# Chunk 0 of a fused layer kernel on one core: identity made by GpSimd, single-block first weights, and two blocks of the first token half moved ahead of the second half's transposes

## The chip, the core and the metric

The kernel runs on one core of a Trainium2 chip. The metric is the device time in microseconds (us) of one execution. The engines are PE (TensorE), DVE (VectorE), ACT (ScalarE), POOL (GpSimd) and SP (SyncE, which here issues nearly all DMAs).

## The reference

`x` is (2, 4096, 256) float32. It is normalised over its last axis to `xn` (no scale, no shift), and

```
out = x + branch(xn) + gelu(xn @ w1 + b1) @ w2 + b2
```

with `w1` 256x1024, `w2` 1024x256. The branch is a spectral filter along the 256 features whose coefficients come from one number (a fractal dimension of the first 1024 values of `xn`), followed by a 24-bit latent code that is corrected and projected back. In the kernel the filter becomes two small circulant matrices, made once from the fractal dimension.

## The kernel before, in words

The 8192 tokens are 16 chunks of 512. In each chunk the feed-forward part has 8 blocks of 128 hidden units. For block m, `up` (line 861) puts six matmuls of 512 columns into bank `m % 2` of `p_h`: the three terms `w1_hi*xT_hi`, `w1_lo*xT_hi`, `w1_hi*xT_lo`, each over two halves k of the features. ACT makes `h` from that bank (gelu, line 428) and its rounded part `h_hi` (line 436), DVE the rest `h_lo` (line 606), and `down` (line 891) sums into `p_f` with four matmuls for `h_hi` (line 904) and two for `h_lo` (line 909). Block m + 2 needs its bank free: `up` waits for `gelu_done` of block m. Every operand is split so into a rounded part `hi` (made by ACT) and a remainder `lo` (made by DVE after `hi`).

All engines' programs are written out by hand in order; each engine does what stands there, waiting on semaphores. Chunk 0 is a start of its own:

- SP issues, in order: three loads of the first rows of `x` (line 238), the identity (line 289), the first part of `w1` (blocks 0 and 1, line 242 through `load_w1(0)`), then the small inputs, the second part of `w1`, the constants, the first part of `w2`, the `x` of chunk 1, the last parts of `w1` and `w2`, the basis, and others. Then it waits in `spread_rows(1)` (lines 268 to 287) for POOL's reciprocal deviations of chunk 1, writes them and the means to DRAM (line 275, `rows_dram`) and reads them back, broadcast to all partitions (line 286, `rows_sb`).
- POOL clears a few tiles, `ones` among them (line 330), then makes the reciprocal deviations of chunk 0 in two halves of tokens (lines 346 and 351).
- DVE: statistics of the first rows (lines 750 to 762), `normalise(0)` and `normalise(1)` (line 743, into `xn0`, which is the memory of a `rows_sb`), `w1_part_lo(0)` (line 730), then `xT_lo` of both halves (line 765), `w1_part_lo(1)`, the first step of the fractal dimension (lines 777 to 781), `hidden_lo(0, 0)`, `w2_part_lo(0)` (line 736), more of the dimension (lines 785 to 788), `w1_part_lo(2)`, `hidden_lo(0, 1)`, and then the statistics of chunk 1 (line 564).
- ACT: `w1_part_hi(0)` (line 476), `xT_hi` of both halves (line 487), `w1_part_hi(1)`, then gelu and `h_hi` of block 0, `w2_part_hi(0)`, gelu and `h_hi` of block 1, `w1_part_hi(2)`, gelu of block 2 and so on.
- PE: 12 matmuls on zeros (line 1052), the wait for the identity, for each half of the tokens four transposes of 128x128 (line 1059) into `p_s`, then `up` of blocks 0 to 3. Block 0 is cut in two halves of 256 columns, all three terms of the first half ahead of those of the second. After block 2 stands a small sum for the fractal dimension (line 1046). Then `down` of block m and `up` of block m + 4 take turns.

Chunk 1 (`first_branch_chunk`) starts the branch; on PE its second group of latents (line 930) needs the bits of chunk 0 taken by DVE (line 611). From there the chunks repeat in a loop.

Of the kernel before, what the change touches and what calls it, by code (L numbers as in the profile page):

```python
# [8 lines left out]
ALU = mybir.AluOpType  # L9
# [11 lines left out]
HF = E // 2  # L21
HR = 4
BANK = 512
W1_PARTS = ((0, 2), (2, 4), (4, 6), (6, MB))
W1_LOADS = ((0, 2), (2, 4), (4, MB))
W2_PARTS = ((0, 2), (2, 4), (4, MB))
W2_LOADS = ((0, 4), (4, MB))
# [38 lines left out]
S_END = S_WEL + KB * LAT  # L66


def build(nc, x, xt, small, latent, w1, w2, ident, consts, basis, codes, out):
    ctx = ExitStack()  # L70
    with ctx:
        def sb(name, shape, dt):
# [5 lines left out]
        def sem(name):  # L78
            return ctx.enter_context(nc.semaphore(name))
# [91 lines left out]
        rows_in = [sem("rows_in_even"), sem("rows_in_odd")]  # L171
        w1_in = [sem(f"w1_in{i}") for i in range(len(W1_LOADS))]
        w2_in = [sem(f"w2_in{i}") for i in range(len(W2_LOADS))]
        id_in, con_in, basis_in, small_in = sem("id_in"), sem("con_in"), sem("basis_in"), sem("small_in")
        code_in, latent_in, stored = sem("code_in"), sem("latent_in"), sem("stored")
        idle_set, pool_set, word_set, cw_set, le_set = (sem("idle_set"), sem("pool_set"), sem("word_set"),
                                                        sem("cw_set"), sem("le_set"))
# [56 lines left out]
        def _(sp):  # L234
# [51 lines left out]
                sp.dma_start(rows_sb[par][:, :, :].rearrange("p a t -> p (a t)"),  # L286
                             rows_dram[par].rearrange("a t -> (a t)").partition_broadcast(P)).then_inc(rows_in[par], 16)

            sp.dma_start(id_sb[:], ident).then_inc(id_in, 16)
            load_w1(0)  # L290
            sp.dma_start(small_sb[:], small).then_inc(small_in, 16)
            load_w1(1)
# [33 lines left out]
        @block.gpsimd  # L326
        def _(pool):
            nc.gpsimd.memset(eps[:], LN_EPS).then_inc(pool_set, 1)
            nc.gpsimd.memset(minus_half[:], -0.5).then_inc(pool_set, 1)
            nc.gpsimd.memset(ones[:], 1.0).then_inc(pool_set, 1)  # L330
            nc.gpsimd.memset(cw[:].bitcast(F32), 0.0).then_inc(cw_set, 1)
            nc.gpsimd.memset(le3[:], 0.0).then_inc(le_set, 1)
            pool.wait_ge(pool_set, 3)
            links = [0]

            def then(ins):

                links[0] += 1
                ins.then_inc(pool_link, 1)
                pool.wait_ge(pool_link, links[0])  # L340

            def inverse_root(step, par, tiles=slice(0, CT), mean=True):


                pool.wait_ge(stat_done, step + 1)
                nc.gpsimd.tensor_tensor(var_eps[:, tiles], mv[par][:, tiles, 1], eps[:, tiles],  # L346
                                        ALU.add).then_inc(veps_done, 1)
                if mean:
                    nc.gpsimd.tensor_copy(row_nums[par][:, 0, tiles], mv[par][:, tiles, 0]).then_inc(mean_done, 1)
                pool.wait_ge(veps_done, step + 1)  # L350
                nc.gpsimd.tensor_tensor(row_nums[par][:, 1, tiles], var_eps[:, tiles], minus_half[:, tiles],  # L351
                                        ALU.pow).then_inc(rstd_done, 1)

            def turn(c):

                pool.wait_ge(scaled, c)
                pool.wait_ge(u_lo, c)
                for k, op in enumerate((ALU.add, ALU.subtract)):
                    nc.gpsimd.tensor_tensor(uv[:, k, :], xn[:, 0, :], xn[:, 1, :], op).then_inc(turned, 1)  # L359


            for g in range(2):
                inverse_root(g, 0, slice(g * HALF, (g + 1) * HALF), mean=False)
            inverse_root(1 + HEAD, 1)


            pool.wait_ge(angle_made, 1)
            wide = [P, PAIRS, COLS]
            t, s, s2, s4 = angle[:, :], powers[:, 0, :], powers[:, 1, :], powers[:, 2, :]
            odd = con[:, K_ODD:K_ODD + PAIRS * COLS].rearrange("p (n c) -> p n c", c=COLS)  # L370
            even = con[:, K_EVEN:K_EVEN + PAIRS * COLS].rearrange("p (n c) -> p n c", c=COLS)
            then(nc.gpsimd.tensor_tensor(s, t, t, ALU.mult))
            nc.gpsimd.tensor_tensor(s2, s, s, ALU.mult)
            then(nc.gpsimd.tensor_tensor(quads[:], odd, s.unsqueeze(1).broadcast_to(wide), ALU.mult))
            nc.gpsimd.tensor_tensor(s4, s2, s2, ALU.mult)
            then(nc.gpsimd.tensor_tensor(quads[:], quads[:], even, ALU.add))
            by_two = quads[:].rearrange("p (n two) c -> p n two c", two=2)
            nc.gpsimd.tensor_tensor(weighted[:], t, con[:, K_WK:K_WK + COLS], ALU.mult)
            then(nc.gpsimd.tensor_tensor(halves2[:], by_two[:, :, 1, :], s2.unsqueeze(1).broadcast_to([P, 2, COLS]),
                                         ALU.mult))  # L380
            then(nc.gpsimd.tensor_tensor(halves2[:], halves2[:], by_two[:, :, 0, :], ALU.add))
            then(nc.gpsimd.tensor_tensor(series[:], halves2[:, 1, :], s4, ALU.mult))
            then(nc.gpsimd.tensor_tensor(series[:], series[:], halves2[:, 0, :], ALU.add))
            then(nc.gpsimd.tensor_tensor(series[:], series[:], weighted[:], ALU.mult))
            nc.gpsimd.tensor_tensor(filt_w[:], series[:, 0:KB], series[:, KB:2 * KB], ALU.mult).then_inc(filt_made, 1)

            inverse_root(2 + HEAD, 0)
            turn(1)
            with pool.Fori(0, (CHUNKS - 4) // 2) as i:
                for u in range(2):  # L390
                    turn(2 * i + 2 + u)
                    inverse_root(2 * i + 3 + u + HEAD, 1 - u)
            turn(CHUNKS - 2)
            inverse_root(CHUNKS - 1 + HEAD, 1)
            turn(CHUNKS - 1)

        @block.scalar
        def _(act):
# [83 lines left out]


            w1_part_hi(0)
            for g in range(2):
                act.wait_ge(t0_done, g + 1)
                nc.scalar.copy(half_tokens(xT_hi[0], g), half_bank(g)).then_inc(t0_hi, 1)
            w1_part_hi(1)
            act.wait_ge(small_in, 16)
            gelu(0, 0, first=True)  # L490
            hidden_hi(0, 0, first=True)
            w2_part_hi(0)
            gelu(0, 1, first=True)
            hidden_hi(0, 1, first=True)
            w1_part_hi(2)
            gelu(0, 2, first=True)
            hidden_hi(0, 2, first=True)
            w2_part_hi(1)
            w1_part_hi(3)
            gelu(0, 3, first=True)  # L500
            hidden_hi(0, 3, first=True)
            w2_part_hi(2)
# [44 lines left out]
        def _(dve):  # L547
# [209 lines left out]
            last.then_inc(stats_made, 1)  # L757
            dve.wait_ge(stats_made, 2)
            aggregate(0, range(HALF, CT))
            for g in range(2):  # L760
                normalise(g)
            w1_part_lo(0)
            for g in range(2):
                dve.wait_ge(t0_hi, g + 1)
                nc.vector.tensor_tensor(half_tokens(xT_lo[0], g), half_bank(g), half_tokens(xT_hi[0], g).bitcast(F32),  # L765
                                        ALU.subtract).then_inc(t0_lo, 1)


            table = [P, NS, FRE]
# [1 line left out]
            logs = con[:, K_CLOG:K_CLOG + NS * FRE].rearrange("p (s f) -> p s f", f=FRE)  # L771
            numbers = con[:, K_NUM:K_NUM + FRE].unsqueeze(1).broadcast_to(table)
            values = fr_v[:, :].unsqueeze(1).broadcast_to(table)
            w1_part_lo(1)

            first_rows = p_s[:, :, :].rearrange("p g (a t) -> p (g a) t", t=P)[:, :, 0]
            nc.vector.tensor_copy(fr_v[:, :], first_rows).then_inc(fr_taken, 1)
# [8 lines left out]
            then(nc.vector.tensor_tensor(fr_b[:], values, fr_s[:, 1, :].unsqueeze(2).broadcast_to(table), ALU.is_gt))  # L786
            then(nc.vector.tensor_tensor(fr_a[:], fr_b[:], masks, ALU.mult))
            nc.vector.tensor_reduce(fr_s[:, 2, :], fr_a[:], AX.X, ALU.add).then_inc(part_counts, 1)
            w1_part_lo(2)
            hidden_lo(0, 1)  # L790
            statistics(1, 1)
            dve.wait_ge(stats_made, 3)
# [5 lines left out]
            then(nc.vector.tensor_tensor(fr_a[:], fr_b[:], logs, ALU.mult))  # L798
            nc.vector.tensor_reduce(fr_d[:, 0:1], fr_a[:].rearrange("p s f -> p (s f)"), AX.X,
                                    ALU.add).then_inc(logged, 1)  # L800
            w1_part_lo(3)
            w2_part_lo(1)
            hidden_lo(0, 3)
            dve.wait_ge(dim_made, 1)
# [53 lines left out]
        def _(pe):  # L858
            mm = nc.tensor.matmul

            def up(c, par, m, first=False):
# [4 lines left out]
                for n, (m0, _) in enumerate(W1_PARTS):  # L866
                    if first and m == m0:

                        pe.wait_ge(*((w1_hi_ready, 1) if n == 0 else (w1_ready, n + 1)))
                if not (first and m < 2):  # L870

                    pe.wait_ge(gelu_done, MB * c + m - 1)

                groups = 2 if first and m == 0 else 1
                for g in range(groups):
                    tok = slice(g * CTOK // groups, (g + 1) * CTOK // groups)
                    n = 0
                    for w, xp in ((w1_hi, xT_hi), (w1_lo, xT_hi), (w1_hi, xT_lo)):
                        if groups == 2:

                            if w is w1_lo and g == 0:
                                pe.wait_ge(w1_ready, 1)
                            elif w is w1_hi:
                                pe.wait_ge(t0_hi if xp is xT_hi else t0_lo, g + 1)
                        for k in range(KB):
                            last = mm(p_h[:, m % 2, tok], w[:, k, m * P:(m + 1) * P], xp[par][:, k, tok],  # L886
                                      start=(n == 0), stop=(n == 3 * KB - 1))
                            n += 1
                last.then_inc(up_done, 1)

            def down(c, m, first=False):

# [157 lines left out]
            pe.wait_ge(idle_set, 1)  # L1050
            for _ in range(IDLE):
                mm(p_f[:, 0, :], idle[:, 0:P], idle[:], start=True, stop=True)
            pe.wait_ge(id_in, 16)
            for g in range(2):

                pe.wait_ge(xn0_done, g + 1)
                for k in range(KB):
                    for j in range(HALF):
# [1 line left out]
                                                   xn0[:, g * HALF + j, k * P:(k + 1) * P], id_sb[:])  # L1060
                last.then_inc(t0_done, 1)

            pe.wait_ge(pool_set, 3)
            for m in range(LOOK):
                up(0, 0, m, first=True)
                if m == 2:
                    summed_over(0, NS, fr_s[:, 0, :], part_sums, fr_summed)
# [21 lines left out]
def constants():  # L1089
# [52 lines left out]
    for par in range(2):  # L1142
# [4 lines left out]
        fixed[2 * SEG, :, 0:LAT] = 9.5  # L1147
        fixed[ROWS:ROWS + SYN, :, 0:SYN] = (1.0 - 13.0 * np.eye(SYN))[:, None, :]
        codes[:, par, 0:ROWS] = fixed.reshape(P, ROWS)
    return np.eye(P, dtype=f4), con, basis, codes.reshape(P, 2 * P)  # L1150


def layouts(inputs):
# [37 lines left out]
```

## Time and profile before

| | us |
|---|---|
| median of 3 runs | 414.21 |
| the three runs | 413.71, 414.21, 415.49 |
| the profiled execution, its own time | 413.36 |
| span of the profiled execution | 411.5 |
| time around the span (413.36 - 411.5) | 1.86 |
| TensorE clock granted, mean of the span | 1.0 of full |

Times in the rows are from the start of the span. "Idle before" is the time in which an engine had nothing to do ahead of the instruction, with what released it. Back-to-back instructions of ACT and DVE overlap by about 0.1 us in the records, since the next starts while the last drains: a group's us are from its first start to its last end.

### The profile page before, as it was taken

How to read it: one execution, taken by the hardware profiler on the slowest of the kernel's cores; microseconds unless marked ns; L12 is line 12 of the kernel's file. 1: busy time of each engine (PE TensorE's matmuls, PEld its weight loads, DVE VectorE, ACT ScalarE, POOL GpSimd, SP SyncE). 2: the span in 40 equal slices, each digit the busy share in tenths (PEclk: the TensorE clock that was granted, in tenths of full speed). 3: DMA queues.
4: the chain of work that ended last, by engine and by line, in shares of the span. 5: the costliest groups of instructions: out<-in, count | busy, mean ns of one | idle time of the engine just before them, and what ended most of it. 6: DMA issues, size and time to landing. Idle time of an engine off the chain costs nothing.

```text
span 411.5 us, 5561 instructions
## 1 busy us (share of the span) xinstructions
PE 405.6 (99%) x1785; PEld 325.0 (79%) x1785; DVE 308.8 (75%) x505; ACT 218.4 (53%) x325; POOL 71.8 (17%) x100
## 2 busy tenths in 40 slices
PE   8999999999999999999999999999999999999996
PEld 4887788888878878788887878888788887878874
DVE  7889986868678686876968778686786868676654
ACT  3966536555454655536555454655536654464541
POOL 2143301212012121201212012121111212012000
PEclk9999999999999999999999999999999999999999
DMA  7544233222323113233113333213333111111011
GB/s 214 187 155 154 102 104 102 59 51 97 104 102 102 37 66 102 102 102 101 49 55 102 102 102 101 34 69 102 102 102 101 52 51 51 52 52 53 0 51 51
DMA packets 16495, 35.78 MB, mean 87 GB/s; under 512 B 5452, under 2 KB 8164, under 8 KB 16484
## 3 DMA queue, kind: packets, MB, share of 16 engines
q1 hardware_dynamic: 16340, 35.52, 27.0%
q10 hardware_dynamic: 144, 0.13, 0.1%
q8 instruction: 5, 0.08, 0.1%
q14 instruction: 6, 0.05, 0.0%
HBM read 27.19 MB, written 8.45 MB: 87 GB/s over the span
## 4 chain that ended last, share of the span: by engine, by line
PE 91%; DVE 4%; DMA 2%; POOL 1%; issue 1%; ACT 1%; SPq 0%; DVEq 0%; POOLq 0%
PE p_h L886 40%; PE p_f L904 26%; PE p_f L909 13%; PE p_s L941 5%; PE p_l L930 3%; PE p_s L960 2%; DMA rows_sb<-rows_dram 1%; PE p_g L954 1%; DMA x_sb<-x 1%; DMA rows_dram<-row_nums 1%; DVE stats L564 1%; POOL row_nums L351 1%; DVE h_lo L606 0%; DVE xn L586 0%; DVE xn L591 0%
## 5 line engine op out<-in xcount | busy, mean ns | idle before, releaser
L428 ACT ACTIVATE h<-p_h,small_sb 128x512 f32<-128x512 f32 x128 | 88.0, 688 | 155.4 <-PE p_h L886 155.3
L606 DVE TENSOR_TENSOR h_lo<-h,h_hi 128x512 fp32r<-128x512 f32 x128 | 90.1, 705 | 66.8 <-ACT h_hi L436 66.6
L904 PE MATMUL p_f<-h_hi,w_hi 128*128 128x512 f32 x254 | 99.3, 391 | 0.0
L904 PE MATMUL p_f<-h_hi,w_lo 128*128 128x512 f32 x254 | 98.9, 389 | 0.0
L886 PE MATMUL p_h<-xT_hi,w_hi 128*128 128x512 f32 (+1 forms) x258 | 85.7, 413 | 0.1
L436 ACT CAST h_hi<-h 128x512 fp32r<-128x512 f32 x128 | 79.5, 621 | 5.8
L886 PE MATMUL p_h<-xT_hi,w_lo 128*128 128x512 f32 (+1 forms) x258 | 79.4, 389 | 0.0
L886 PE MATMUL p_h<-xT_lo,w_hi 128*128 128x512 f32 (+1 forms) x258 | 79.1, 388 | 0.0
L909 PE MATMUL p_f<-h_lo,w_hi 128*128 128x512 f32 x254 | 78.2, 389 | 0.0
L359 POOL TENSOR_TENSOR uv<-xn 128x512 f32<-128x512 f32 x30 | 44.5, 1502 | 127.2 <-DVE xn L591 127.2
L886 PEld LDWEIGHTS p_h<-xT_lo,w_hi 128*128 128x128 f32 x258 | 48.3, 188 | 10.5 <-DVE xT_lo L765 0.2
L886 PEld LDWEIGHTS p_h<-xT_hi,w_lo 128*128 128x128 f32 x258 | 48.3, 188 | 10.2
L886 PEld LDWEIGHTS p_h<-xT_hi,w_hi 128*128 128x128 f32 x258 | 48.4, 189 | 10.1 <-issue 0.3
L909 PEld LDWEIGHTS p_f<-h_lo,w_hi 128*128 128x128 f32 x254 | 47.7, 188 | 10.1
L904 PEld LDWEIGHTS p_f<-h_hi,w_hi 128*128 128x128 f32 x254 | 47.7, 188 | 10.0
L904 PEld LDWEIGHTS p_f<-h_hi,w_lo 128*128 128x128 f32 x254 | 47.7, 188 | 9.9
L346 POOL TENSOR_TENSOR var_eps<-mv,eps 128x4 f32<-128x4 f32 (+1 forms) x17 | 3.8, 222 | 171.0 <-DVE mv L569 171.0
L596 DVE TENSOR_TENSOR xT_lo<-xn,xT_hi 128x1024 fp32r<-128x1024 f32 x15 | 32.7, 2179 | 0.5 <-ACT xT_hi L406 0.5
L630 DVE SCALAR_TENSOR_TENSOR xt_sb<-p_f,bias,xt_sb 128x512 f32 (+1 forms) x30 | 21.1, 745 | 12.3 <-PE p_f L909 12.3
L601 DVE TENSOR_TENSOR uv_lo<-uv,uv_hi 128x1024 fp32r<-128x1024 f32 x16 | 19.6, 1227 | 6.1 <-ACT uv_hi L413 6.1
L586 DVE TENSOR_TENSOR xn<-xt_sb,rows_sb 128x1024 f32<-128x1024 f32 x15 | 18.4, 1225 | 7.6 <-DMA rows_sb<-rows_dram 4.2
L406 ACT CAST xT_hi<-xn 128x1024 fp32r<-128x1024 f32 x15 | 15.8, 1054 | 15.3 <-DVE xn L591 15.3
(115 smaller groups left out, 326.5 us busy)
## 6 DMA issues: line engine op xcount, KB each, us to landing
xt_sb<-xt SPq DMA_DIRECT2D x16, 512.0 KB, 5.3
x_sb<-x SPq DMA_DIRECT2D x15, 512.0 KB, 4.7
rows_sb<-rows_dram SPq DMA_DIRECT2D x15, 512.0 KB, 4.4
out<-xt_sb SPq DMA_DIRECT2D x15, 512.0 KB, 2.9
xt_sb<-w SPq DMA_DIRECT2D x3, 512.0 KB, 7.6
xt_sb<-w SPq DMA_DIRECT2D x2, 256.0 KB, 4.5
x_sb<-x SPq DMA_DIRECT2D x2, 128.0 KB, 2.4
x_sb<-x SPq DMA_DIRECT2D x1, 256.0 KB, 3.0
```

The costliest lines, as they stand in the source:

```text
L359: nc.gpsimd.tensor_tensor(uv[:, k, :], xn[:, 0, :], xn[:, 1, :], op).then_inc(turned, 1)
L428: nc.scalar.activation(h[m % 2][:], p_h[:, m % 2, :], ACT.Gelu, bias=small_sb[:, S_B1 + m:S_B1 + m + 1]).then_inc(gelu_done, 1)
L436: nc.scalar.copy(h_hi[m % HR][:], h[m % 2][:]).then_inc(h_hi_done, 1)
L586: nc.vector.tensor_tensor(xn[:, :, :], columns(c), to_halves(rows_sb[par][:, 0, :]), ALU.subtract).then_inc(centred, 1)
L596: nc.vector.tensor_tensor(xT_lo[par][:, :, :], xn[:, :, :], xT_hi[par][:, :, :].bitcast(F32), ALU.subtract).then_inc(t_lo, 1)
L601: nc.vector.tensor_tensor(uv_lo[:, :, :], uv[:, :, :], uv_hi[:, :, :].bitcast(F32), ALU.subtract).then_inc(u_lo, 1)
L606: nc.vector.tensor_tensor(h_lo[m % HR][:], h[m % 2][:], h_hi[m % HR][:].bitcast(F32), ALU.subtract).then_inc(h_lo_done, 1)
L630: nc.vector.scalar_tensor_tensor(out=xc, in0=p_f[:, k, :], scalar=bias[:, k:k + 1], in1=xc, op0=ALU.add, op1=ALU.add).then_inc(ffn_added, 1)
L886: last = mm(p_h[:, m % 2, tok], w[:, k, m * P:(m + 1) * P], xp[par][:, k, tok], start=(n == 0), stop=(n == 3 * KB - 1))
L904: mm(p_f[:, a, :], w[:, m, a * HF:(a + 1) * HF], h_hi[r][:], start=(m == 0 and w is w2_hi), stop=False, skip_group_check=True)
L909: last = mm(p_f[:, a, :], w2_hi[:, m, a * HF:(a + 1) * HF], h_lo[r][:], start=False, stop=(m == MB - 1), skip_group_check=True)
L941: last = mm(p_s[:, k, :], w[:, k, :], xp[:, k, :], start=(n == 0), stop=False, skip_group_check=True)
```

## The change

SP no longer loads an identity; POOL makes it from `ones` with an `affine_select` of 128x128 after its clearing. The first part of `w1` (still one load) is rounded in two parts of one block each. On PE, the first half of the tokens is transposed, then the first two terms of block 0 on that half, then the second half is transposed, then the rest of block 0 and all of block 1 on the first half, then both blocks on the second half. On DVE, `w1_part_lo(0)` moves in between `normalise(0)` and `normalise(1)`, and the new `w1_part_lo(1)` stands between the `xT_lo` of the two halves.

```diff
-W1_PARTS = ((0, 2), (2, 4), (4, 6), (6, MB))
+W1_PARTS = ((0, 1), (1, 2), (2, 4), (4, 6), (6, MB))
...
-            sp.dma_start(id_sb[:], ident).then_inc(id_in, 16)
             load_w1(0)
...
             pool.wait_ge(pool_set, 3)
+
+            nc.gpsimd.affine_select(out=id_sb[:], in_=ones[:], pattern=[[1, P]], base=0, channel_multiplier=-1,
+                                    compare_op=ALU.is_equal, fill=0.0).then_inc(id_made, 1)
...
             w1_part_hi(0)
+            w1_part_hi(1)
             for g in range(2):
                 act.wait_ge(t0_done, g + 1)
                 nc.scalar.copy(half_tokens(xT_hi[0], g), half_bank(g)).then_inc(t0_hi, 1)
-            w1_part_hi(1)
+            w1_part_hi(2)
...
-            for g in range(2):
-                normalise(g)
+            normalise(0)
             w1_part_lo(0)
+            normalise(1)
             for g in range(2):
                 dve.wait_ge(t0_hi, g + 1)
                 nc.vector.tensor_tensor(half_tokens(xT_lo[0], g), half_bank(g), half_tokens(xT_hi[0], g).bitcast(F32),
                                         ALU.subtract).then_inc(t0_lo, 1)
+                if g == 0:
+                    w1_part_lo(1)
...
+            def half_up(m, g, terms):
+
+                tok = slice(g * GTOK, (g + 1) * GTOK)
+                for n in terms:
+                    w, xp = ((w1_hi, xT_hi), (w1_lo, xT_hi), (w1_hi, xT_lo))[n]
+                    for k in range(KB):
+                        last = mm(p_h[:, m, tok], w[:, k, m * P:(m + 1) * P], xp[0][:, k, tok],
+                                  start=(n == 0 and k == 0), stop=(n == 2 and k == KB - 1))
+                return last
...
-            pe.wait_ge(id_in, 16)
+            pe.wait_ge(id_made, 1)
...
+            turn_rows(0)
+            pe.wait_ge(w1_hi_ready, 1)
+            pe.wait_ge(t0_hi, 1)
+            half_up(0, 0, (0,))
+            pe.wait_ge(w1_ready, 1)
+            half_up(0, 0, (1,))
+            turn_rows(1)
+            pe.wait_ge(t0_lo, 1)
+            half_up(0, 0, (2,))
+            pe.wait_ge(w1_ready, 2)
+            half_up(1, 0, (0, 1, 2))
+            pe.wait_ge(t0_hi, 2)
+            half_up(0, 1, (0, 1))
+            pe.wait_ge(t0_lo, 2)
+            half_up(0, 1, (2,)).then_inc(up_done, 1)
+            half_up(1, 1, (0, 1, 2)).then_inc(up_done, 1)
+
             pe.wait_ge(pool_set, 3)
-            for m in range(LOOK):
+            for m in range(2, LOOK):
                 up(0, 0, m, first=True)
```

The other parts of `w1` keep their places under numbers one higher, and `up` of block 0 loses its own cut in two.

## Rows read from the trace of the kernel before

**Rows 1.** The profile's page: busy us, share of the span and instructions of each engine.

```profile
PE 405.6 (99%) x1785; PEld 325.0 (79%) x1785; DVE 308.8 (75%) x505; ACT 218.4 (53%) x325; POOL 71.8 (17%) x100
```

**Rows 2.** The chain that ended last, first 40 us: start us, us, what.

```profile
13.12 0.13 PE p_g L1046 x2
...
13.28 0.18 DVE fr_s L785
...
15.43 1.32 DVE stats L564 x4
...
21.53 4.40 DMA rows_sb<-rows_dram
...
37.98 1.20 PE p_l L930 x4
```

**Rows 3.** Who waited for whom, first 45 us: us in total, times, longest.

```profile
PE p_l L930 <- DVE word L611: 0.4, 1, 0.4
```

**Rows 4.** Timeline of PE: start us, us, engine, line, operation, count, idle before.

```profile
6.74 0.63 PE L1059 MATMUL p_s<-id_sb,rows_sb 128*128 128x128 f32 x4 [0.33 <-DVE rows_sb L743]
7.65 0.66 PE L1059 MATMUL p_s<-id_sb,rows_sb 128*128 128x128 f32 x4 [0.29 <-DVE rows_sb L743]
8.41 0.48 PE L886 MATMUL p_h<-xT_hi,w_hi 128*128 128x256 f32 x2
...
9.74 0.40 PE L886 MATMUL p_h<-xT_hi,w_lo 128*128 128x256 f32 x2
9.97 0.40 PE L886 MATMUL p_h<-xT_lo,w_hi 128*128 128x256 f32 x2
...
11.60 0.61 PE L886 MATMUL p_h<-xT_hi,w_hi 128*128 128x512 f32 x2
...
13.10 0.70 PE L886 MATMUL p_h<-xT_hi,w_hi 128*128 128x512 f32 x2
```

**Rows 5.** Timeline of ACT, the same columns.

```profile
7.16 0.62 ACT L476 CAST w_hi<-xt_sb 128x512 fp32r<-128x512 f32 x1 [4.93 <-DMA xt_sb<-w]
7.68 1.25 ACT L487 CAST xT_hi<-p_s 128x512 fp32r<-128x512 f32 x2
...
10.48 0.69 ACT L428 ACTIVATE h<-p_h,small_sb 128x512 f32<-128x512 f32 x1 [1.03 <-PE p_h L886]
...
12.24 0.68 ACT L428 ACTIVATE h<-p_h,small_sb 128x512 f32<-128x512 f32 x1
...
29.76 0.38 ACT L525 CAST c_hi<-p_l 128x256 fp32r<-128x256 f32 x1
```

**Rows 6.** Timeline of DVE, the same columns.

```profile
6.18 0.41 DVE L743 TENSOR_SCALAR rows_sb<-x_sb,mv,row_nums 128x256 f32<-128x256 f32 x1
6.86 0.73 DVE L743 TENSOR_SCALAR rows_sb<-x_sb,mv,row_nums 128x256 f32<-128x256 f32 x2 [0.27 <-POOL row_nums L351]
7.81 0.69 DVE L730 TENSOR_TENSOR w_lo<-xt_sb,w_hi 128x512 fp32r<-128x512 f32 x1 [0.21 <-ACT w_hi L476]
8.42 1.28 DVE L765 TENSOR_TENSOR xT_lo<-p_s,xT_hi 128x512 fp32r<-128x512 f32 x2
...
11.85 0.69 DVE L606 TENSOR_TENSOR h_lo<-h,h_hi 128x512 fp32r<-128x512 f32 x1 [1.01 <-ACT h_hi L436]
...
31.97 0.42 DVE L836 TENSOR_TENSOR c_lo<-c_f,c_hi 128x256 fp32r<-128x256 f32 x1
```

**Rows 7.** Timeline of SP's queue, the same columns.

```profile
2.11 0.43 SPq L289 DMA_DIRECT2D id_sb<-ident  x1
2.58 0.43 SPq L242 DMA_DIRECT2D xt_sb<-w  x1
```

**Rows 8.** Groups of POOL by form: busy us, mean ns | idle before us, releaser.

```profile
L351 POOL TENSOR_TENSOR row_nums<-var_eps,minus_half 128x4 f32<-128x4 f32 x15 | 15.3, 1019 | 0.0
...
L351 POOL TENSOR_TENSOR row_nums<-var_eps,minus_half 128x2 f32<-128x2 f32 x2 | 1.5, 736 | 0.2
...
L346 POOL TENSOR_TENSOR var_eps<-mv,eps 128x2 f32<-128x2 f32 x2 | 0.4, 196 | 3.3 <-DVE mv L569 3.3
...
L330 POOL MEMSET ones<- 128x128 f32 x1 | 0.2, 205 | 0.0
```

More of the change, by code:

```diff
@@ L66, with build @@
 S_END = S_WEL + KB * LAT
-def build(nc, x, xt, small, latent, w1, w2, ident, consts, basis, codes, out):
+def build(nc, x, xt, small, latent, w1, w2, consts, basis, codes, out):
     ctx = ExitStack()
@@ L173, in build @@
         w2_in = [sem(f"w2_in{i}") for i in range(len(W2_LOADS))]
-        id_in, con_in, basis_in, small_in = sem("id_in"), sem("con_in"), sem("basis_in"), sem("small_in")
+        id_made, con_in, basis_in, small_in = sem("id_made"), sem("con_in"), sem("basis_in"), sem("small_in")
         code_in, latent_in, stored = sem("code_in"), sem("latent_in"), sem("stored")
@@ L494, in _ @@
             hidden_hi(0, 1, first=True)
-            w1_part_hi(2)
+            w1_part_hi(3)
             gelu(0, 2, first=True)
@@ L498, in _ @@
             w2_part_hi(1)
-            w1_part_hi(3)
+            w1_part_hi(4)
             gelu(0, 3, first=True)
@@ L773, in _ @@
             values = fr_v[:, :].unsqueeze(1).broadcast_to(table)
-            w1_part_lo(1)
+            w1_part_lo(2)
             first_rows = p_s[:, :, :].rearrange("p g (a t) -> p (g a) t", t=P)[:, :, 0]
@@ L788, in _ @@
             nc.vector.tensor_reduce(fr_s[:, 2, :], fr_a[:], AX.X, ALU.add).then_inc(part_counts, 1)
-            w1_part_lo(2)
+            w1_part_lo(3)
             hidden_lo(0, 1)
@@ L800, in _ @@
                                     ALU.add).then_inc(logged, 1)
-            w1_part_lo(3)
+            w1_part_lo(4)
             w2_part_lo(1)
@@ L867, in up @@
                     if first and m == m0:
-                        pe.wait_ge(*((w1_hi_ready, 1) if n == 0 else (w1_ready, n + 1)))
+                        pe.wait_ge(w1_ready, n + 1)
                 if not (first and m < 2):
                     pe.wait_ge(gelu_done, MB * c + m - 1)
[L874 to L888, printed above, removed]
-                last.then_inc(up_done, 1)
+                n = 0
+                for w, xp in ((w1_hi, xT_hi), (w1_lo, xT_hi), (w1_hi, xT_lo)):
+                    for k in range(KB):
+                        last = mm(p_h[:, m % 2, :], w[:, k, m * P:(m + 1) * P], xp[par][:, k, :],
+                                  start=(n == 0), stop=(n == 3 * KB - 1))
+                        n += 1
+                last.then_inc(up_done, 1)
+            def half_up(m, g, terms):
+                tok = slice(g * GTOK, (g + 1) * GTOK)
+                for n in terms:
+                    w, xp = ((w1_hi, xT_hi), (w1_lo, xT_hi), (w1_hi, xT_lo))[n]
+                    for k in range(KB):
+                        last = mm(p_h[:, m, tok], w[:, k, m * P:(m + 1) * P], xp[0][:, k, tok],
+                                  start=(n == 0 and k == 0), stop=(n == 2 and k == KB - 1))
+                return last
             def down(c, m, first=False):
@@ L1052, in _, with turn_rows @@
                 mm(p_f[:, 0, :], idle[:, 0:P], idle[:], start=True, stop=True)
-            pe.wait_ge(id_in, 16)
-            for g in range(2):
+            pe.wait_ge(id_made, 1)
+            def turn_rows(g):
                 pe.wait_ge(xn0_done, g + 1)
@@ L1149, in constants @@
         codes[:, par, 0:ROWS] = fixed.reshape(P, ROWS)
-    return np.eye(P, dtype=f4), con, basis, codes.reshape(P, 2 * P)
+    return con, basis, codes.reshape(P, 2 * P)
 def layouts(inputs):
@@ L1178 @@
     arrays = {name: np.ascontiguousarray(a) for name, a in layouts(inputs).items()}
-    for name, a in zip(("ident", "consts", "basis", "codes"), constants()):
+    for name, a in zip(("consts", "basis", "codes"), constants()):
         arrays[name] = a
```

## The prediction

> **What bounds the kernel now.** I read the page's busy shares first: PE is busy for 405.6 of 411.5 us [rows 1], so a change of chunk 0 can only matter by what it does to the few waits before the steady part. Next the chain that ended last, in order of time [rows 2]. It leaves PE at 13.25 us, after block 2 and the small sum for the fractal dimension: DVE work, from 13.28 to the statistics of chunk 1 at 15.43, then the trip of the row numbers through DRAM (the read back alone 4.40 us, landing at 25.93), more DVE, and back to PE at 37.98 us. From there PE carries it nearly alone. In the list of waits PE's idle time at that place is 0.4 us, for DVE's bits of chunk 0 [rows 3]. So from 13.3 to 38 us it is DVE's chain, not PE's, that sets the end, with PE only 0.4 us ahead of it. Whatever delays DVE at 13 to 15 us goes into the time in full; whatever PE gains there is lost in the wait at 38 us.
>
> Then, by the timelines, what starts DVE's chain. At 11.85 DVE begins `hidden_lo(0, 0)` after 1.01 us of idling for ACT's `h_hi` [rows 6]; behind it stand `w2_part_lo(0)` and then the step of 13.28, which PE's sum (over at 13.25) released at the same moment [rows 2]. ACT in turn begins the gelu of block 0 at 10.48 after 1.03 us of idling for PE [rows 5], and from there works without a gap (the gelu of block 1 follows at 12.24, with two casts between, and its later casts feed `w1_part_lo(2)` and `hidden_lo(0, 1)`, which DVE has between 13.28 and 15.43). So ACT from 10.48 on is a solid line, and **the number that decides is when PE completes block 0**: its last two matmuls start at 9.97 and end at 10.37, ACT starts 0.11 later [rows 4, 5].
>
> **The change part by part.**
>
> *Identity load gone.* Each DMA behind it leaves SP 2.58 - 2.11 = 0.47 us earlier [rows 7]. Only one is waited for: the first part of `w1`, for which ACT idles until 7.16 [rows 5]. Its landing can come between 0 us (if the transfers ahead of it set it) and 0.47 us earlier; I take 0.4, as it stands right behind the identity in the queue, so ACT starts at 6.76. Everything behind gains the same and nobody waits for it.
>
> *Identity by GpSimd.* The trace has no `affine_select`. From below the nearest row is the clearing of `ones`, 0.2 us for the same 128x128; from above the power function, whose 736 ns for two columns and 1019 ns for four make 0.14 us a column, 18 us for 128 [rows 8]. The cover is POOL's idle time of 3.3 us before its first `var_eps` [rows 8]: PE needs the identity only at 6.7. I take a cost of nothing: a select has no function to evaluate and is nearest the clearing. POOL takes no more than 3.3 us unless it goes by the power function's price, which is kept as a rival. The Trainium skill speaks against using this engine: "GPSIMD Engine Reference", section "Elementwise — side-by-side cycle accounting", gives about 12 cycles an element where code branches on data; by its 1.2 GHz that would be an estimated 1.3 us here, which no row shows and which the cover would still hide.
>
> *Single blocks.* ACT's cast of 512 columns takes 0.62 and steps by 0.52 (7.16 to 7.68); one of 256 takes 0.38 [rows 5], and steps by about 0.3. Two of them: 6.76 and 7.06, ends 7.15 and 7.45. ACT is free for the first `xT_hi` at 7.36; the first transposes end at 7.37 as before [rows 4]. So `xT_hi` of the first half runs 7.41 to 7.99, where it was 7.68 to 8.26: 0.27 gained.
>
> *DVE's order.* `normalise(0)` ends at 6.18 + 0.41 = 6.59 [rows 6]. `w1_part_lo(0)`, now ahead of `normalise(1)`, waits for ACT until 7.15 and takes 0.42 (the row of 256 columns [rows 6]), stepping by 0.34. `normalise(1)`, queued behind that wait, runs 7.52 to 8.25 instead of 6.86 to 7.59 [rows 6]: 0.66 later. Who waits: the second transposes. Then `xT_lo` of the first half from 8.17 to 8.85, `w1_part_lo(1)` from 8.77 to 9.19.
>
> *PE.* First half, terms 0 and 1 of block 0: from 8.05 (0.06 after `xT_hi`). A pair of 256-column matmuls steps by 9.97 - 9.74 = 0.23 [rows 4], so they are issued by 8.52. The second transposes go 8.52 to 9.18 (0.66 [rows 4]), against an end of 8.31 before. The next matmul came 0.10 after the transposes' end before (8.31 to 8.41); I take 0.07: 9.25. Term 2 of block 0: to 9.48. Block 1 on the first half: 0.70, to 10.18. Meanwhile ACT makes the second `xT_hi` 9.22 to 9.80 and DVE the second `xT_lo` 9.84 to 10.52; both are ready in time for PE: terms 0 and 1 of block 0's second half to 10.65, and term 2 from 10.65, ending 0.40 after [rows 4] at 11.05. **Block 0 is complete at 11.05 instead of 10.37: 0.68 later.** The reason is plain counting: 18 half matmuls and four transposes now stand between the first `xT_hi` and the end of block 0, where 12 half matmuls did. Block 1 then ends its issue at 11.35, a little ahead of the 11.60 of before (24 half matmuls at 0.117 are 2.8 us either way): PE has filled its gaps, but block 2 cannot use it, since its bank waits for the gelu of block 0: 11.16 + 0.69 = 11.85, then 0.05, so 11.9 against 11.60. Block 3 waits for the gelu of block 1 at 12.24 + 0.68 + 0.68 = 13.60 and starts at 13.65 against 13.10 [rows 4, 5]. PE itself is 0.55 late.
>
> *DVE's chain.* `h_lo` at 11.85 + 0.68 = 12.53, then `w2_part_lo(0)`, so the step of 13.28 comes at about 13.9; the casts that DVE needs next come 0.68 later too. Chunk 1's statistics move from 15.43 to 16.1, POOL idles before its next turn so nothing absorbs it, SP sends the numbers when POOL is done, and the return to PE moves from 37.98 to 38.65. PE's 0.55 fits under it (its wait there grows from 0.44 to 0.57).
>
> **Sum.** -0.27 (`xT_hi` sooner, from the load and the smaller cast) and +0.95 (six more half matmuls, 0.70, and the transposes with their joint, 0.76, ahead of block 0's end, less the 0.5 of waits on PE that go) = +0.68 on DVE's chain, taken as +0.7. Against the profiled execution: 413.36 + 0.7 = 414.1 (span 412.2). The median lay 0.85 above that execution, so the forecast is 414.21 + 0.7 = **414.9**. The unknowns: a `w1` landing at the full 0.47 changes nothing below +0.6, as the first transposes then set the start; with faster joints +0.4 is the low end. With no earlier landing all steps after 7.4 come 0.35 later: +1.05. About 0.5% (2.1 us) is what a measurement of this kernel tells from no change.
>
> **The rivals.**
>
> *1. The delay is absorbed (chance 0.17).* Between 15 and 38 us something not in my chain, such as the landing of the row numbers among the other loads, would set DVE's pace. Against it: the read back lies on the chain itself [rows 2] and is issued only when the numbers are there. For it: 4.40 us for such a transfer is long enough to hide a queue. Time: +0, 414.2.
>
> *2. The overlap works (0.08).* If the first part of `w1` landed far sooner and the joints vanished, PE's filled gaps would count: block 1 done 0.25 to 0.5 us earlier. It needs block 0 complete by 10.37, for which PE would have to begin its half matmuls before 7.4, when the first transposes end. It could only come by if the wait of 0.4 us at 38 us went as well. Time: 413.8.
>
> *3. The identity becomes the bound, slower (0.03).* If the select goes at the power function's 0.14 us a column, POOL's first `var_eps`, which stands behind it, comes 18 - 3.3 = 14.7 us later [rows 8], and all of chunk 0 with it: 428.9. It decides from a duration of 3.3 us on. Were it between, say 6 us, the loss is 2.7.
>
> *4. The change doesn't do what it says (0.02).* Were the `w1` load not earlier and the second transposes held by another wait yet, PE would only do the same work in another order with +1.5: 415.7.
>
> **How the numbers follow.** The forecast has 0.70; its own range is +0.4 to +1.05, 414.6 to 415.3. Rivals 1 and 2 reach down to 413.8; a median moves by some tenths by itself (the three runs lie between 0.5 below and 1.3 above theirs), so the range is 413.5 to 416.1. All cases but the third lie within 2.1 us of 414.21, so "same" has 0.92; slower by over 0.5% takes the third case and a high draw on the forecast, 0.06; faster 0.02.
>
> **What would show it.** Right: ACT's first cast at 6.7 to 6.8; DVE's second `normalise` near 7.5; the first `xT_hi` near 7.4; the gelu of block 0 near 11.2; PE idle before block 2 and again before block 3; statistics of chunk 1 near 16.1; the latents at 38.6. Wrong: the gelu of block 0 at or before 10.5; a select of over 3.3 us; statistics late but the latents at 38.0 (rival 1).

## The result, and the profile after

| | before | after |
|---|---|---|
| median of 22 runs, us | 413.54 | 414.62 |
| lowest to highest | 412.95 to 415.49 | 413.83 to 415.91 |
| the profiled execution, its own time | 413.36 | 415.85 |
| its span | 411.5 | 414.1 |
| mean granted TensorE clock of its span | 1.000 | 0.996 |

The ratio is 1.0027, 95% interval 1.0019 to 1.0035: slower by 0.8 to 1.45 us, 1.08 by the medians. The forecast was +0.7 us with 0.92 on a change of less than 0.5%. The direction came, the change is 0.27%, and 414.62 lies in the range (413.5 to 416.1). The size was low: 1.08 against 0.70, just above the forecast's own +0.4 to +1.05. That 414.62 is so near the forecast of 414.9 is in part luck: the forecast stood on a median of three runs, 414.21, which was 0.67 above that of 22. The profiled execution is one of the slower ones and shows more than the typical loss, for a reason that comes below. Two executions of the kernel before, timed beside the experiments, took 576 and 698 us at mean clocks of 0.67 and 0.60; they belong to a slow state and stand in no comparison.

The identity first. The timeline of POOL in the changed kernel (start us, us, engine, line, operation, idle before; these columns hold for all timelines here):

```profile
1.61 0.29 POOL L334 TENSOR_SCALAR_AFFINE_SELECT id_sb<-ones 128x128 f32<-128x128 f32 x1
...
6.82 1.08 POOL L353 TENSOR_TENSOR row_nums<-var_eps,minus_half 128x2 f32<-128x2 f32 x1
```

The select took 0.29 us, near the clearing of `ones` [rows 8], five us before PE needs it. The second line is the power function for the second half of the tokens; it comes back below. Next, DVE from 5 to 12 us:

```profile
5.36 0.75 DVE L759 BATCH_NORM_STATS2 stats<-x_sb 128x6 f32<-128x256 f32 x2 [1.20 <-DMA x_sb<-x]
...
6.31 0.70 DVE L746 TENSOR_SCALAR rows_sb<-x_sb,mv,row_nums 128x256 f32<-128x256 f32 x2
6.93 0.42 DVE L733 TENSOR_TENSOR w_lo<-xt_sb,w_hi 128x256 fp32r<-128x256 f32 x1
7.94 0.73 DVE L746 TENSOR_SCALAR rows_sb<-x_sb,mv,row_nums 128x256 f32<-128x256 f32 x2 [0.59 <-POOL row_nums L353]
```

and ACT:

```profile
6.01 0.71 ACT L478 CAST w_hi<-xt_sb 128x256 fp32r<-128x256 f32 x2 [3.72 <-DMA xt_sb<-w]
7.82 0.59 ACT L490 CAST xT_hi<-p_s 128x512 fp32r<-128x512 f32 x1 [1.10 <-PE p_s L1065]
...
10.43 0.59 ACT L490 CAST xT_hi<-p_s 128x512 fp32r<-128x512 f32 x1 [2.02 <-PE p_s L1065]
...
13.02 0.69 ACT L430 ACTIVATE h<-p_h,small_sb 128x512 f32<-128x512 f32 x1 [1.49 <-PE p_h L893]
```

Against [rows 5] the first cast of `w1` starts 1.15 us sooner (6.01 for 7.16), but nobody gains by it. DVE waited 1.20 us for the last rows of `x` and took them at 5.36; it is those rows, not `w1`, that the first transposes now wait for. DVE takes them in before it normalises the first half, so the first transposes are late as well, and `normalise(1)` starts at 7.94, released by POOL's numbers, which took 1.08 us where the kernel before has 0.76 for the same operation (6.07 to 6.83), and not, as I had it, by `w1_part_lo(0)`, which was over at 7.35. Then PE, against [rows 4]:

```profile
7.16 0.63 PE L1065 MATMUL p_s<-id_sb,rows_sb 128*128 128x128 f32 x4 [1.12 <-DVE rows_sb L746]
...
8.55 0.56 PE L893 MATMUL p_h<-xT_hi,w_hi 128*128 128x256 f32 x2 [0.77 <-ACT xT_hi L490]
...
9.34 1.05 PE L1065 MATMUL p_s<-id_sb,rows_sb 128*128 128x128 f32 x4
...
11.05 0.63 PE L893 MATMUL p_h<-xT_hi,w_lo 128*128 128x256 f32 x2
11.48 0.63 PE L893 MATMUL p_h<-xT_lo,w_hi 128*128 128x256 f32 x2
...
12.52 0.40 PE L893 MATMUL p_h<-xT_lo,w_hi 128*128 128x256 f32 x2
12.76 0.40 PE L893 MATMUL p_h<-xT_hi,w_hi 128*128 128x256 f32 x2
```

A pair of half matmuls steps by 0.43 (11.05 to 11.48) where it steps by 0.24 a microsecond later. The windows say why; columns are busy us (instructions) of PE, weight loads, DVE, ACT and POOL, the granted clock, the share and the GB/s of the DMA engines:

```profile
8.00:9.00 1.00, 0.45 (x3) 0.48 (x4) 1.00 (x3) 0.41 (x1) 0.00 (x0) 0.90 1.04 325
9.00:10.00 1.00, 1.00 (x7) 1.00 (x7) 0.60 (x2) 0.00 (x0) 0.00 (x0) 0.50 1.02 385
10.00:12.00 2.00, 2.00 (x11) 2.00 (x10) 0.95 (x2) 1.10 (x2) 0.00 (x0) 0.50 1.04 391
12.00:14.00 2.00, 1.78 (x14) 1.61 (x14) 0.81 (x4) 0.94 (x2) 0.00 (x0) 0.95 1.06 365
```

From about 8.8 to 12.2 us the granted clock is 0.50, the 1.2 GHz level. Ahead of that PE had idled 1.12 us, done four transposes, and idled 0.77 us. From 14 us to the end it is 1.00, the 2.4 GHz level.

Last, the return to PE, in the chain (start us, us, what) and in the list of waits (us in total, times, longest):

```profile
40.57 1.19 PE p_l L936 x4
```

```profile
PE p_l L936 <- DVE word L614: 0.6, 1, 0.6
```

It is at 40.57 for 37.98 [rows 2], 2.59 later; the gelu of block 0 (13.02 for 10.48) is 2.54 later, the span 2.6 longer. PE's wait there grew from 0.4 [rows 3] to 0.6.

### The profile page after: what moved, and what is told of

It is laid out like the page before. It is cut to its first block, busy times and chain, and to the rows that moved or that the text cites. A ratio compares the mean times of both kernels' runs of the same rounds, so it can differ in the third digit from the quotient of the medians.

```text
span 414.1 us, 5560 instructions
## 1 busy us (share of the span) xinstructions
PE 406.7 (98%) x1776; PEld 326.8 (79%) x1791; DVE 308.6 (75%) x506; ACT 218.6 (53%) x326; POOL 74.3 (18%) x101
## 4 chain that ended last, share of the span: by engine, by line
PE 90%; DVE 4%; POOL 2%; ACT 2%; DMA 1%; issue 1%; SPq 0%; DVEq 0%; ACTq 0%
PE p_h L882 39%; PE p_f L910 26%; PE p_f L915 13%; PE p_s L947 5%; PE p_l L936 3%; PE p_s L966 2%; DMA x_sb<-x 1%; PE p_h L893 1%; DVE stats L567 1%; DVE h_lo L609 1%; PE p_s L1065 0%; ACT h L430 0%; DVE w_lo L733 0%; DVE xT_lo L599 0%; DVE uv L839 0%
## 5 line engine op out<-in xcount | busy, mean ns | idle before, releaser
L882 PE MATMUL p_h<-xT_hi,w_hi 128*128 128x512 f32 x252 | 84.3, 415 | 0.2 <-ACT h L430 0.2
L882 PE MATMUL p_h<-xT_hi,w_lo 128*128 128x512 f32 x252 | 77.9, 391 | 0.0
L882 PE MATMUL p_h<-xT_lo,w_hi 128*128 128x512 f32 x252 | 77.6, 389 | 0.0
L882 PEld LDWEIGHTS p_h<-xT_hi,w_hi 128*128 128x128 f32 x252 | 47.4, 189 | 10.1 <-issue 0.4
L882 PEld LDWEIGHTS p_h<-xT_lo,w_hi 128*128 128x128 f32 x252 | 47.3, 188 | 10.2
L882 PEld LDWEIGHTS p_h<-xT_hi,w_lo 128*128 128x128 f32 x252 | 47.3, 188 | 10.1
```

The lines of the kernel that those rows point to most:

```text
L882: last = mm(p_h[:, m % 2, :], w[:, k, m * P:(m + 1) * P], xp[par][:, k, :], start=(n == 0), stop=(n == 3 * KB - 1))
```

## The experiments

Each was timed in turn with the kernel before (9 to 12 runs of each; 32, 34 and 34 of the kernel before, medians 413.58, 413.53 and 413.62 in the three sets). "Fallen" means an execution whose mean clock is under 0.9965; the ratios and medians have all executions in them where nothing else is said. Three questions: does the end of block 0 set the whole time; which part of the change makes it late; what do the clock and the loads add.

**First set.** Edits against the changed kernel, except the last, which is against the kernel before.

`block0_first`: PE completes block 0 before block 1.

```diff
             half_up(0, 0, (2,))
-            pe.wait_ge(w1_ready, 2)
-            half_up(1, 0, (0, 1, 2))
             pe.wait_ge(t0_hi, 2)
             half_up(0, 1, (0, 1))
             pe.wait_ge(t0_lo, 2)
             half_up(0, 1, (2,)).then_inc(up_done, 1)
+            pe.wait_ge(w1_ready, 2)
+            half_up(1, 0, (0, 1, 2))
             half_up(1, 1, (0, 1, 2)).then_inc(up_done, 1)
```

> The changed kernel, but PE completes block 0 (both token halves) before any matmul of block 1. If the loss comes from the late completion of block 0 (theory 1), the gelu of block 0 starts about 0.7 us sooner than in the changed kernel and the median falls by about 0.7 us, to a ratio of 1.0000 to 1.0010 against the kernel before. If the loss comes from TensorE's clock falling in a third of the executions (theory 2), the order of the blocks changes nothing and the ratio stays at 1.0020 or more, with as many executions below a mean clock of 1.0 as in the changed kernel.

Measured 414.65, ratio 1.0043 (1.0022 to 1.0063). My main term was wrong: nothing was gained. Nor is the clock behind that: 5 of 11 executions had fallen, two of them to 0.992 (417.59 and 417.93 us), but the six others have a median of 414.41, where the changed kernel's 15 others have 414.33. The trace shows PE idle where the six half matmuls had stood:

```profile
10.40 0.51 PE L893 MATMUL p_h<-xT_hi,w_hi 128*128 128x256 f32 x2 [0.44 <-ACT xT_hi L490]
```

The second token half arrives too late whatever PE does meanwhile.

`after_warm`: filler work in PE's wait.

```diff
             turn_rows(0)
+            for _ in range(4):
+                mm(p_f[:, 0, 0:GTOK], idle[:, 0:P], idle[:, 0:GTOK], start=True, stop=True)
             pe.wait_ge(w1_hi_ready, 1)
```

> The changed kernel with four more matmuls of 256 columns on zeros behind the first transposes, where PE waits for the first xT_hi. Theory 2 (clock): hardly an execution has a mean clock below 1.0, and the median falls by 0.3 to 0.5 us, the upper tail by 1.3 us. Theory 1 (order): the median stays within 0.2 us of the changed kernel, ratio 1.0020 to 1.0030.

Measured 414.38, ratio 1.0023 (1.0006 to 1.0041). One of 9 executions had fallen, against 7 of 22. The median is 0.24 lower, between what the two theories said, and the interval does not tell it from no change; the eight others have 414.35, the same as the changed kernel's 414.33. So the filler gives back only what the falls cost. Its trace is at full clock and shows what the new order does without a fall:

```profile
8.91 0.60 PE L1065 MATMUL p_s<-id_sb,rows_sb 128*128 128x128 f32 x4
9.26 0.48 PE L893 MATMUL p_h<-xT_lo,w_hi 128*128 128x256 f32 x2
...
10.91 0.50 PE L893 MATMUL p_h<-xT_lo,w_hi 128*128 128x256 f32 x2
```

```profile
10.16 0.69 DVE L768 TENSOR_TENSOR xT_lo<-p_s,xT_hi 128x512 fp32r<-128x512 f32 x1 [0.75 <-ACT xT_hi L490]
```

The second `xT_lo` ends at 10.85, and the last term of block 0, which needs it, follows at 10.91; the gelu follows at 11.52.

`after_id_dma`: the identity by DMA again, at its old place.

```diff
+            sp.dma_start(id_sb[:], ident).then_inc(id_made, 16)
             load_w1(0)
...
-            nc.gpsimd.affine_select(out=id_sb[:], in_=ones[:], pattern=[[1, P]], base=0, channel_multiplier=-1,
-                                    compare_op=ALU.is_equal, fill=0.0).then_inc(id_made, 1)
...
-            pe.wait_ge(id_made, 1)
+            pe.wait_ge(id_made, 16)
```

> The changed kernel with the identity loaded by DMA again, as before the change. If taking that load away lets the first part of w1 compete with the last rows of x (theory 3: in the changed kernel those rows were used from 5.36 us instead of 4.66), the rows come at 4.7 again, the first transposes start near 6.7, w1 arrives near 7.1, and the time falls by 0 to 0.5 us against the changed kernel. If the removed load was the gain that I took it for, the time rises by 0.3 us.

Measured 414.17, ratio 1.0015 (1.0006 to 1.0024): less than the changed kernel, not more, though the two intervals overlap. DVE took the last rows at 4.67, as in the kernel before. None of the 11 executions had fallen; against the changed kernel's 15 at full clock (414.33) the gain is 0.16, and the rest of the 0.45 is the falls that did not come.

`id_only`: the kernel before with only the identity moved to GpSimd.

> The kernel before with the identity made by GpSimd and its load gone, nothing else. By my sum the first w1 cast starts 0.4 us sooner or more, the first xT_hi 0.2 us sooner, ratio 0.9993 to 1.0000. By theory 3 the last rows of x come 0.7 us later, the second transposes with them, and the ratio is 1.0005 to 1.0015.

Measured 413.66, ratio 1.0007 (0.9998 to 1.0017), the last rows of `x` taken at 5.00. The interval holds no change as well as theory 3's loss; the first `xT_hi` gained nothing (7.63 for 7.68).

**Second set.**

`dve_order`: DVE's `normalise(1)` ahead of `w1_part_lo(0)` again.

```diff
             normalise(0)
+            normalise(1)
             w1_part_lo(0)
-            normalise(1)
```

> The changed kernel with DVE's order of before: normalise(1) ahead of w1_part_lo(0). Theory A (what sets the end of block 0 is the chain of the second token half: second transposes, xT_hi, xT_lo; and what delays it is PE's own order, which holds the second transposes behind the first xT_hi): nothing changes within 0.2 us, since PE reaches the second transposes only at about 9 us anyway. Theory B (normalise(1) held by the wait for ACT's first cast is what delays it): the second transposes start 0.4 us sooner and the time falls by 0.4 us.

Measured 414.43, ratio 1.0026 (1.0014 to 1.0038): no change, theory A (the ten executions that had not fallen: 414.30). In its trace `normalise(1)` does start sooner, 2.24 us after the rows of `x` (7.07 after 4.83) instead of 2.59 (7.75 after 5.16 in `after_warm`), but PE comes to the second transposes only at 8.57. The gelu is 0.34 us earlier than `after_warm`, all of it from rows of `x` that came 0.33 sooner.

`together`: this, and both groups of transposes back to back on PE.

```diff
             turn_rows(0)
+            turn_rows(1)
             pe.wait_ge(w1_hi_ready, 1)
             pe.wait_ge(t0_hi, 1)
             half_up(0, 0, (0,))
             pe.wait_ge(w1_ready, 1)
             half_up(0, 0, (1,))
-            turn_rows(1)
             pe.wait_ge(t0_lo, 1)
```

> The changed kernel with both groups of transposes back to back as before, on PE and on DVE (identity by GpSimd, single blocks and both blocks of the first half first stay). Theory A: the second transposes start at about 8.0 us, the gelu of block 0 at 11.0 to 11.3 instead of 11.5, the time falls by 0.3 to 0.5 us, and executions with a fallen clock become rare, since PE no longer idles as long before its first half matmuls. If the six half matmuls of block 1 ahead of block 0's end are the loss, as my sum had it, nothing is gained.

Measured 414.21, ratio 1.0026 (1.0014 to 1.0038). The ratio did not fall, and fallen clocks did not become rare: 5 of 12. The seven others have a median of 414.08 where the changed kernel's 15 others have 414.33: 0.25 less, which is small beside the scatter of these few executions.

`together_first_dma`: `together`, `block0_first` and the identity's load in one.

> As the last, and block 0 completed ahead of block 1, and the identity loaded by DMA: of the change only the single-block weights and a block 1 cut in halves stay. Theory A with the x rows in time (theory 3): the gelu of block 0 starts at 10.3 to 10.6 as in the kernel before, ratio 0.9993 to 1.0007.

Measured 413.56, ratio 1.0006 (0.9997 to 1.0014); the gelu of block 0 at 10.62, 0.02 above what was expected, with the rows of `x` at 4.92. The whole loss is gone within what can be told.

`id_small_first`: `id_only`, and the small inputs loaded ahead of the first `w1`.

```diff
-            load_w1(0)
             sp.dma_start(small_sb[:], small).then_inc(small_in, 16)
+            load_w1(0)
```

> The kernel before with the identity by GpSimd, and the load of the small inputs put ahead of the first part of w1, where the identity's load stood. Theory 3 (w1 moved up competes with the last rows of x): those rows are used from 4.7 us as before, w1 arrives near 7, ratio 0.9993 to 1.0003, that is 0.2 to 0.3 us less than with the identity's load merely gone (1.0007). Against it: the rows still come at 5.0 or later.

Measured 413.64, ratio 1.0007 (0.9994 to 1.0020). In the trace the theory is right (rows at 4.68, `w1` cast at 7.13, span 411.3, the shortest of all), in the time nothing is shown.

**Third set.**

`together_first`: `together` and `block0_first`, identity by GpSimd.

> Transposes back to back as before and block 0 completed ahead of block 1, identity still by GpSimd. If the order of the transposes and the six half matmuls of block 1 are two delays of about 0.6 us side by side (each hides the other, so undoing one alone gained nothing), both are gone here: the gelu of block 0 starts 5.7 us after DVE takes the last rows of x, as in the kernel before (5.8), where the changed order needs 6.4. Ratio 1.0005 to 1.0015, the rest being the later rows of x. If only the identity's load made the difference in the run with it, the ratio stays at 1.002.

Measured 413.81, ratio 1.0001 (0.9992 to 1.0009), better than expected in the ratio. Its one trace is of an execution with a fallen clock (0.996), so its interval from the rows to the gelu, 6.61, can't be compared.

`together_first_small`: as the last, small inputs first.

> As together_first, with the load of the small inputs ahead of the first part of w1. If w1 moved up is what makes the last rows of x late, they come at 4.7 us and the ratio is 0.9990 to 1.0005, the best of all versions. If not, it equals together_first.

Measured 413.72, ratio 1.0001 (0.9989 to 1.0012): no better, so whether the small load's place is worth anything stays open. The rows came at 4.59, but `w1` at 7.80, so here ACT waited for `w1`:

```profile
7.80 0.71 ACT L478 CAST w_hi<-xt_sb 128x256 fp32r<-128x256 f32 x2 [5.51 <-DMA xt_sb<-w]
```

`together_warm`: `together` with four filler matmuls between the two groups of transposes.

> The run with the transposes back to back, in which 5 of 12 executions had a mean clock of 0.996, with four matmuls of 256 columns on zeros between the two groups of transposes. If PE's idling there makes the clock fall, 0 to 2 of 12 executions fall and the median is 414.1. If the fall has another cause, 3 to 6 of 12 fall.

Measured 414.20, ratio 1.0011 (1.0001 to 1.0021): 0 of 11 executions fell, the highest 414.61 where `together` had 415.87. The two were timed in different sets, but in this set `after_small_first`, without filler, fell in 4 of 11.

`after_small_first`: the changed kernel, small inputs first.

> The changed kernel with the load of the small inputs ahead of the first part of w1. Theory 3 for the changed kernel: the last rows of x come at 4.7 us instead of 5.36, w1 near 6.9 as with the identity's load kept, and the median falls to that run's 414.2 (ratio 1.0015). If the place of w1 in the queue does not matter, it stays at 1.0025.

Measured 414.57, ratio 1.0030 (1.0013 to 1.0046). The rows came at 4.62, as expected, and `w1` at 6.48, sooner than the 6.9 expected; the median did not fall: 4 of 11 executions had the fallen clock (median 416.13, the seven others 414.43).

**All traces side by side** (us, one execution each: when DVE takes the last rows of `x`, when ACT starts on `w1`, when the second transposes and the gelu of block 0 start):

| kernel | rows of x | w1 | 2nd transposes | gelu 0 | span | gelu - rows | span - gelu |
|---|---|---|---|---|---|---|---|
| before | 4.66 | 7.16 | 7.65 | 10.48 | 411.5 | 5.82 | 401.0 |
| id_small_first | 4.68 | 7.13 | 7.71 | 10.44 | 411.3 | 5.76 | 400.9 |
| id_only | 5.00 | 5.69 | 8.04 | 10.71 | 411.9 | 5.71 | 401.2 |
| together_first_dma | 4.92 | 6.54 | 7.95 | 10.62 | 411.7 | 5.70 | 401.1 |
| together_warm | 5.05 | 5.76 | 8.10 | 11.16 | 412.1 | 6.11 | 400.9 |
| dve_order | 4.83 | 5.50 | 8.57 | 11.18 | 412.1 | 6.35 | 400.9 |
| after_warm | 5.16 | 5.85 | 8.91 | 11.52 | 412.6 | 6.36 | 401.1 |
| block0_first | 5.38 | 6.12 | 9.13 | 11.74 | 412.9 | 6.36 | 401.2 |
| after_small_first | 4.62 | 6.48 | 8.37 | 10.98 | 412.1 | 6.36 | 401.1 |
| after_id_dma | 4.67 | 6.91 | 8.79 | 11.40 | 412.3 | 6.73 | 400.9 |
| together_first_small | 4.59 | 7.80 | 7.63 | 11.32 | 412.3 | 6.73 | 401.0 |
| together_first, fallen clock | 5.33 | 6.04 | 8.37 | 11.94 | 413.2 | 6.61 | 401.3 |
| together, fallen clock | 5.17 | 5.85 | 8.21 | 12.66 | 414.1 | 7.49 | 401.4 |
| after, fallen clock | 5.36 | 6.01 | 9.34 | 13.02 | 414.1 | 7.66 | 401.1 |

The last column is the finding that carries the rest: whatever was done to the first 13 us, the span ended 400.9 to 401.4 us after the gelu of block 0 began.

The columns before it show what makes that gelu late. In the five traces at full clock with the changed order on PE (`dve_order`, `after_warm`, `block0_first`, `after_small_first`, `after_id_dma`) it starts 2.61 us after the second transposes, to the hundredth, with block 1 ahead of block 0's end or behind it. So there it is the second half's own chain that sets it. The second transposes in turn start 3.74 or 3.75 us after the rows of `x` in four of the five (4.12 in `after_id_dma`, where `w1` is late), and 3.03 to 3.05 after them in `id_only`, `together_first_dma` and `together_warm`, where they are back to back. Each row is one execution, and when the rows of `x` come moves by some tenths between executions.

And the executions by clock. A mean does not say where the clock fell; the three traces of fallen executions (`after`, `together`, `together_first`) have the 0.50 from between 8.4 and 8.8 us to about 12 and 1.00 from 12.5 us on:

| kernels | fallen |
|---|---|
| before (the three sets) | 0 of 32, 0 of 34, 0 of 34 |
| after | 7 of 22 |
| block0_first, dve_order, together, after_small_first | 5 of 11, 2 of 12, 5 of 12, 4 of 11 |
| after_id_dma | 0 of 11 |
| after_warm, together_warm | 1 of 9, 0 of 11 |
| id_only, id_small_first | 1 of 12, 1 of 11 |
| together_first, together_first_dma, together_first_small | 2 of 12, 1 of 11, 1 of 12 |

In the changed kernel the 7 have a median of 415.63, the 15 others 414.33: a fall costs 1.3 us. One of the two counted for `together_first` has a mean of 0.949 and took only 414.10 us, so it is no such fall. The traces fit: from the rows of `x` to the gelu it is 7.66 us in the changed kernel's fallen execution and 6.36 in `after_warm`; in 3.4 us at half clock PE gets through what takes it 1.7 at full clock, and a part of the difference lies in waits.

## Why the prediction was right, and where it was wrong

- **"The number that decides is when PE completes block 0": shown.** The span less the gelu's start is the same within 0.5 us in 14 kernels, over a spread of 2.6 us in that start.
- **"+0.68 on DVE's chain, taken as +0.7": near for executions with the full clock, but by another sum, so in part by luck.** The 15 such executions have a median of 414.33, 0.8 above 413.54. In traces, from before to `after_warm`, the gelu moves by 1.04: 0.50 since the rows of `x` come later, 0.65 by the order on PE (6.36 from rows to gelu where `id_only` has 5.71), less 0.11 since `w1` is no longer waited for (5.71 for 5.82).
- **The term "six more half matmuls, 0.70": wrong as a term.** Undoing it alone (`block0_first`) left 6.36 us from rows to gelu, the same as with it. The second token half's own chain, second transposes, `xT_hi`, `xT_lo`, ended at the same time: PE holds the second transposes behind its wait for the first `xT_hi`. In the sum both ran beside each other and I had even written that `xT_lo` was ready at 10.52 for a use at 10.65; I should have read from this that removing the matmuls would gain 0.13. Undoing the transposes alone gained 0.25 (`together_warm`, 6.11), both together 0.66 (`together_first_dma`, 5.70).
- **The term "the transposes with their joint, 0.76": right in place, wrong in size.** That the second transposes now come later is what costs the time. But they hold PE for 0.35 us (8.91 to 9.26 in `after_warm`), not 0.76: the 8.41 in the kernel before is 0.15 after the end of `xT_hi`, which PE waited for, as its 8.55 in the changed kernel is 0.14 after that end. With 0.35 in the sum PE would have been ready for the last term some tenths earlier, and the second `xT_lo` (10.52) alone would have set the end. The total came out because my sum had the two paths only 0.13 apart.
- **The term "-0.27, `xT_hi` sooner": did not come.** The first `xT_hi` started at 7.82 in the changed kernel, 7.63 in `after_warm` and 7.85 in `block0_first`, against 7.68 before and 7.41 forecast. I took the identity's load to be only in the way of `w1`. `w1` did come sooner, by more than the 0.47 that I had as the most. But it then ran beside the last rows of `x`: over the eight traces in which `w1` follows those rows at once they were taken at 4.83 to 5.38, mean 5.16; over the six in which a smaller load stands between, at 4.59 to 4.92, mean 4.69. So the first transposes were late, which my sum held fixed at 6.74 to 7.37. What this costs in the median is not settled: restoring the load gained 0.45 in the changed kernel, of which 0.16 is left among executions at full clock, and moving the small load there gained nothing, though its one trace has the rows in time. In the kernel before, taking the load away cost nothing that can be told (1.0007, 0.9998 to 1.0017).
- **"`normalise(1)`, queued behind that wait": not the cause.** The new order does make it about 0.35 later after the rows of `x`, but PE is not there yet, and `dve_order` changed nothing in the time. In the changed kernel POOL's numbers released it. They were late themselves: this operation took 1.08 or 1.09 us in the three traces in which `w1_part_lo(0)` runs beside it (`after`, `after_warm`, `block0_first`) and 0.75 or 0.76 in the eleven others. That the one slows the other is argued from this alone.
- **Block 2 waits for the gelu, and PE's wait at 38 us grows from 0.44 to 0.57: the waits are there, the growth is not clear.** The list of waits has 0.2 before block 2. For the bits the fallen execution has 0.6, but the traces at full clock have 0.54 (`after_warm`) and 0.42 (`dve_order`).
- **What the sum left out: the clock.** My timeline left PE idle from 7.37 to 8.05 us and asked only when it was ready again. In a third of the executions TensorE's clock fell; where a trace shows it, it fell to the 1.2 GHz level right behind that idle time. That is about 0.4 us on the mean, and 0.29 of the 1.08 in the median (414.62 against 414.33). Filler in the idle time makes it rare (1 of 20 executions with it, 12 of 34 in the two kernels without). The Trainium skill, "TensorE: Matmul & The Clock Gate", section "HAM oscillation — how this bites in real kernels", warns of gaps in PE's work as the cause of such falls; the gaps here, 1.12 and 0.77 us, were shorter than the waits of its example, and a fall came all the same. The same two gaps stand in the trace of `dve_order`, whose clock stayed at 1.00. Why `after_id_dma`, with gaps of 1.07 and 1.06 us, had no fall in 11 stays open.
- **The rivals.** Absorbed (0.17): no, the last column of the table excludes it. The overlap works (0.08): no; PE filled its gaps and waited for the gelu. The identity as the bound (0.03): no, the select took 0.29 us, also far below the prediction's estimate of 1.3. The change not doing what it says (0.02): no; `w1` came sooner, and the second transposes stood behind the wait that the new order gives them.

No version beat the kernel before. The best, with its orders of transposes and blocks restored, equal it: 1.0001 (0.9992 to 1.0009, `together_first`) and 1.0006 (0.9997 to 1.0014, `together_first_dma`), where the changed kernel has 1.0027 (1.0019 to 1.0035). So the new order, with the falls that come with it, is shown as the cause of the loss; how it divides to the hundredth is read from single traces.

## What to carry to other kernels

Find the first handoff that a solid line of work hangs on (here the first gelu) and judge a reordering by that one time; filling PE's gaps with work that the next engine is not waiting for delays it. When two delays run beside each other, undoing one shows nothing: undo both before a cause is dismissed. Taking a load out of a queue moves the others up, also against the one ahead of them that everything waits for.

## What the runs showed of the hardware that was not expected

- An `affine_select` of 128x128 float32 on GpSimd took 0.29 us, hardly more than the 0.20 of a clearing.
- With a DMA of 256 KB issued right behind them on the same queue, the last rows of `x` were taken 0.47 us later, on the mean of eight traces against six in which a load of 30 or 64 KB stood between. The two groups overlap (4.83 the lowest of the one, 4.92 the highest of the other).
- A power function on GpSimd took 1.08 us instead of 0.75 in the three traces in which a subtraction of DVE with two inputs ran beside it.
- TensorE fell to 1.2 GHz in a start with idle stretches of about 1 us each, in some executions of the same program and not in others (7 of 22); with four matmuls of 256 columns on zeros in the idle time it was 1 of 20.
